# An adaLN transformer block planned by slots: GpSimd counted in the plan, one q product moved to the prologue, two stages of one unit later, fillers removed

## The chip, the cores and the metric

The kernel runs on one core of one Trainium2 chip. The time is the device time of one execution in microseconds, lower is better. Times "before" are the median of three runs. Engines: TensorE (PE, with its weight loads as PEld), VectorE (DVE), ScalarE (ACT), GpSimd (POOL), and SyncE (SP), which only issues DMAs here.

## What is computed

One block on x of shape (2, 1024, 128), 16 heads of 8 columns, a router over 8 experts with 64 hidden columns each:

```python
mod = (silu(c) @ wmod).reshape(2, 6, 1, 128)      # sa, ca, ga, sb, cb, gb; ga and gb kept away from 0
h = layernorm(x) * (1 + ca) + sa
q, k, v = heads(h @ qkv_w + qkv_b); q, k = rotary(q), rotary(k)
a = softmax(mask(q @ k.T / sqrt(8))) @ v           # causal
x = x + ga * (a @ out_w + out_b)
h = layernorm(x) * (1 + cb) + sb
onehot = one_hot(argmax(h @ w_router.T), 8)
u = leaky(h @ w_fc) ** 2                           # leaky: slope 0.5 below zero
x = x + gb * sum_e onehot_e * (u_e @ w_proj_e)
```

## The kernel before

The rows are cut into four units (b, half) of 512 rows, computed in the order (0,0), (0,1), (1,1), (1,0). Attention works on steps: a unit times a group of 4 heads, 16 steps in all. Step s has two passes. Pass A (`pass_a`, L968 and L973) makes score banks of 128 x 512 with q as rows, and VectorE reduces each to row maxima (`tmax`, L808). At the end of a step stage `max1` joins them (L738), GpSimd splits the negated maxima into three bf16 parts (`negp`, L486 to L489), and stage `max2` transposes these (PE L891), copies them (ACT L574) and writes them by three DMAs as extra rows of `qst`. Pass B (`pass_b`, L990) then makes the transposed scores with the maximum already subtracted, ScalarE takes the exponential (`exp`, L619), GpSimd zeroes the future of the diagonal tiles (`zero_future`, L515), and TensorE multiplies by v (`times_v`, L1010). Steps of a unit with half = 0 have 11 pass A banks, those with half = 1 have 27.

Before a unit's attention stand its preparation stages (`norm1`, `var1`, `nz`, `hT`, `q1` to `q3`, `k1` to `k3`, `v`, `load`): layer norm, transposition, the q and k products (PE L880), the rotation on VectorE (`rot`, L717), and `split`, which sums the two rotated parts (L355) and cuts the sum into three bf16 parts (L360 and L365, with copies on ScalarE at L562 and L566 between them). SyncE stores the parts to device memory after `q3` and `k3`, and `load` fetches them in the layout of the passes. After a unit's attention stand `n0` to `n3` (transpose and divide), `oT` and `out` (output product), `st` to `ln` (second layer norm), `h2`, `rt` (router), `a0` to `a3`, `m0` to `m3` and `y0`, `y1` (experts). `gates` (L494 to L496) multiplies the gates into the weights on GpSimd once, `xb` (L503) adds the gated bias to x there.

The function `plan` gives each pass A bank, each pass B bank and each stage a slot number. Every engine walks through the slots in order, and each stage issues its part in every engine's program, so a stage's slot is its place in each queue. TensorE does a stage one slot early. `put` moves a stage to a later slot when more than SIDES banks would be held; PREP_AT and POST_AT set starting slots by hand. The stages in `PRE` run ahead of slot 0. All passes and stages share seven PSUM banks in one round. Carried out for before, the plan puts pass A banks on slots 0 to 303 and pass B banks on slots 19 to 338.

`keep_warm` issues matmuls whose result nobody reads (L952, called fillers below): in the prologue, one in each slot before the first pass B bank, one in each slot of 304 to 338 (after the last pass A bank), and some in the last stages:

```python
if i < min(b_at):
    keep_warm(1)
...
if i > max(a_at) and i in b_at:
    keep_warm(1)
```

In unit (0,0) GpSimd does `split` for q and VectorE for k; in the other units GpSimd does both.

Of the kernel before, what the change touches and what calls it, by code (L numbers as in the profile page):

```python
# [29 lines left out]
P = 128  # L30
# [5 lines left out]
HALF = T // 2  # L36
# [35 lines left out]
def groups_b(half):  # L72
# [11 lines left out]
LEAD = 8  # L84
PVLAG = 3
SIDES = 2


HOLD = {"q1": 3, "k1": 3, "max2": 1}
BANKS_OF = {"mod": 1, "gate": 1, "hT": 1, "q1": 2, "k1": 2, "v": 1, "max2": 1, "oT": 1, "out": 1, "h2": 1, "rt": 1,  # L90
            "ohT": 1, "y0": 1, "y1": 1, **{f"n{g}": 1 for g in range(NG)}, **{f"a{c}": 1 for c in range(4)},
# [4 lines left out]
        "m2": 2, "y0": 1, "m3": 3, "y1": 4}  # L96

POST_LAST = ["oT", "out", "st", "var2", "ln", "h2", "rt", "a0", "a1", "ohT", "m0", "a2", "m1", "a3", "m2", "y0", "m3", "y1"]
PREP_AT = [[0, 0], [40, 1], [90, 1]]
POST_AT = {("out", (0, 0)): 79, ("a0", (0, 0)): 131}  # L100
MAX_LAG = 3
O_LAG = 3
GATES_AT = 22


WARM_PRE = {"start": 7, "mod": 8, "hT": 4, "v": 30}
# [1 line left out]
HIDDEN = ("a0", "a1", "a2", "a3")  # L108


PRE = [("mod", 0)] + [(name, (0, 0)) for name in ["norm1", "var1", "nz", "hT", "q1", "k1", "q2", "q3", "k2", "k3", "v"]] \
    + [("load", (0, 0), g) for g in range(NG)] + [(name, (0, 1)) for name in ["norm1", "var1", "nz", "hT"]] \
    + [("gate", 0)]


def plan():

    a_at, a_end, n = {}, [], 0
    for s, (b, half, g) in enumerate(STEPS):
        for job in bank_jobs_a(half):  # L120
            a_at[n] = (s, job)
            n += 1
        a_end.append(n)
    b_at, v_at, stages, held = {}, {}, {}, {}
    slot, v_end = 0, []
    for s, (b, half, g) in enumerate(STEPS):
        slot = max(slot, a_end[s] + LEAD)
        for gi, grp in enumerate(groups_b(half)):
            for bank in grp[3]:
                b_at[slot] = (s, gi, grp, bank, bank is grp[3][-1])  # L130
                slot += 1
            v_at[slot - 1 + PVLAG] = (s, gi, grp)
        v_end.append(slot - 1 + PVLAG)

    def put(at, *stage):

        need, hold = BANKS_OF.get(stage[0], 0), HOLD.get(stage[0], 2)
        if need and stage[0] in HIDDEN + ("y0", "y1") and stage[1][0:2] == UNITS[-1]:
            hold = 1
        while need and any(held.get(t, 0) + need > SIDES for t in range(at, at + hold)):  # L140
            at += 1
        for t in range(at, at + hold if need else at):
            held[t] = held.get(t, 0) + need
        stages.setdefault(at, []).append(stage)
        return at

    for s in range(len(STEPS)):
        put(a_end[s] - 1, "max1", s)
        put(a_end[s] + MAX_LAG, "max2", s)
        put(v_end[s], "o", s)  # L150
    put(GATES_AT, "gates", 0)
    done = {}
    for u, (at, more) in zip(PREPS[1:], PREP_AT):
        for name, gap in PREP.items():
            if (name, u) not in PRE:
                at = put(at + gap + more, name, u)
                if name == "k3":
                    done[u] = at
    for g in range(NG):
        at = a_end[1 + g] + MAX_LAG  # L160
        assert at > done[(0, 1)]
        put(at, "load", (0, 1), g)
        at = max(a_end[6 + g] + MAX_LAG, done[(1, 1)] + 1)
        assert v_end[4 + g] < at < a_end[7 + g] - LEAD
        for half in range(2):
            put(at, "load", (1, half), g)
    for s, (b, half, g) in enumerate(STEPS):
        at = put(v_end[s] + O_LAG, f"n{g}", (b, half))
        if g == 2:
            put(at + 1, "xb", (b, half))  # L170
        if g == NG - 1:
            for name in POST if (b, half) != UNITS[-1] else POST_LAST:
                at = max(at + POST[name], POST_AT.get((name, (b, half)), 0))
                for piece in range(len(PIECES[(b, half)])):
                    at = put(at, name, (b, half, piece))
    slots = max(list(a_at) + list(b_at) + list(v_at) + list(stages)) + 1
    return slots, a_at, b_at, v_at, stages, a_end


def adaln_block(nc, x, ct, wmod, wqkv, wsw, bcol, bv, wo, bo, wr, wfc, wpj, rope, out):  # L180
    slots, a_at, b_at, v_at, stages, a_end = plan()
# [24 lines left out]
    with ExitStack() as ctx:  # L206
# [6 lines left out]
        def sem(name):  # L213
            return ctx.enter_context(nc.semaphore(name))
# [7 lines left out]
        bv_sb = sb("bv_sb", [P, D])  # L222
# [66 lines left out]
        s_ldx = [sem(f"s_ldx{i}") for i in range(B * 2)]  # L289
        s_ldct, s_ldmod, s_ldqkv, s_ldbv = sem("s_ldct"), sem("s_ldmod"), sem("s_ldqkv"), sem("s_ldbv")  # L290
        s_ldrest = sem("s_ldrest")
        s_ident, s_mask, s_consts = sem("s_ident"), sem("s_mask"), sem("s_consts")
        s_one, s_ones, s_vones = sem("s_one"), sem("s_ones"), sem("s_vones")
        s_pool = sem("s_pool")
# [74 lines left out]
        def _(sp):  # L369
# [1 line left out]
            sp.dma_start(wqkv_sb[:, :], wqkv).then_inc(s_ldqkv, 16)  # L371
            sp.dma_start(wsw_sb[:, :], wsw).then_inc(s_ldqkv, 16)
            sp.dma_start(bcol_sb[:, :], bcol).then_inc(s_ldqkv, 16)
            sp.dma_start(rope_sb[:, :, :], rope).then_inc(s_ldqkv, 16)
            sp.dma_start(bv_sb[:, :], bv.partition_broadcast(P)).then_inc(s_ldbv, 16)
            for i in range(1, B * 2):
                sp.dma_start(xs[:, i], x[i]).then_inc(s_ldx[i], 16)
            sp.dma_start(bo_sb[:, :], bo.partition_broadcast(P)).then_inc(s_ldrest, 16)
# [56 lines left out]
        def _(pool):  # L435
# [36 lines left out]
            def run(st):  # L472
                name, u = st[0], st[1]
                if name in ("var1", "var2"):
                    rstd_of(st)
                if st == ("v", (0, 0)):
                    router_consts()
                if name in ("q1", "q2", "q3") or name in ("k1", "k2", "k3") and prep_no[u]:
                    split(pool, name, u)
                if name == "max1":  # L480
                    s, par = u, u % 2
# [149 lines left out]
        def _(dve):  # L631
# [58 lines left out]
            def run(st):  # L690
# [18 lines left out]
                if name in ("q1", "k1"):  # L709
                    i = (0, 1)[name == "k1"]  # L710
                    if name == "q1" and prep_no[u] == 0:
                        dve.wait_ge(s_ldqkv, 64)
                    if prep_no[u]:
                        dve.wait_ge(s_part[i], 3 * prep_no[u])
                    for j in range(2):
                        src, free = side_ready(dve, st, j)
                        dve.scalar_tensor_tensor(out=rot[i][:, j], in0=src, scalar=bcol_sb[:, 2 * i + j:2 * i + j + 1],  # L717
                                                 in1=rope_sb[:, j, HALF * u[1]:HALF * u[1] + HALF],
                                                 op0=ALU.add, op1=ALU.mult).then_inc(free, 1)
                if name in ("k1", "k2", "k3") and prep_no[u] == 0:  # L720
                    split(dve, name, u)
                if name == "v":
                    w = TU * (2 * u[0] + u[1])
# [90 lines left out]
        def _(pe):  # L814
# [30 lines left out]
            def run(st):  # L845
# [27 lines left out]
                if name in ("q1", "k1"):  # L873
                    i = (0, 1)[name == "k1"]
                    if i == 0:
                        pe.wait_ge(s_ldqkv, 64)
                    wait_read(pe, "hT", u)
                    for j, w in enumerate((wqkv_sb, wsw_sb)):
                        dst, full_ = fill(st, j)
                        pe.matmul(dst, w[:, D * i:D * i + D], ht[:, :], start=True, stop=True).then_inc(full_, 1)  # L880
# [139 lines left out]
            for i in range(slots):  # L1020
# [5 lines left out]
                    keep_warm(1)  # L1026
                if i in v_at:
                    times_v(*v_at[i])
                if i > max(a_at) and i in b_at:
                    keep_warm(1)  # L1030
                for st in pe_at.get(i, []):
                    run(st)
                    if i > max(b_at) and st[0] in WARM_POST:
# [48 lines left out]
```

## Time and profile before

| what | value |
|---|---|
| median of 3 runs | 392.32 us (389.57, 392.32, 393.1) |
| profiled execution | 389.84 us, span of its instructions 388.1 us |
| PE busy | 348.0 us (90% of the span) |
| DVE busy | 258.3 us (67%) |
| ACT busy | 215.9 us (56%) |
| POOL busy | 100.7 us (26%) |
| mean granted TensorE clock | 0.965 |
| chain that ended last | PE 68%, DVE 6%, issue 6%, POOL 6%, ACT 2% |

An engine's busy time says how much work it had, not whether it set the end. The granted clock is the share of TensorE's full speed that it was given: 1.00 is 2.4 GHz and 0.50 is 1.2 GHz. In a timeline the bracket at the end of a row is the idle time before it and what ended that.

### The profile page before, as it was taken

The page shows a single profiled execution, that of the slowest core. Times are in us where ns is not written, and L with a number is a line of the kernel's source. Part 1 is how long each engine was busy: PE and PEld are TensorE (multiplying, and loading weights), DVE is VectorE, ACT ScalarE, POOL GpSimd, SP SyncE. Part 2 cuts the span into 40 slices and gives each one's busy share as a digit, 9 for nine tenths or more (in the row PEclk, how much of TensorE's full clock was granted, in tenths as well). Part 3 has the DMA queues.
Part 4 walks back from the last instruction along what each step waited for, and adds up shares of the span by engine and source line. Part 5 has one row for each costly group of instructions (what it writes and reads, how often), then busy time and mean ns, then how long its engine had stood idle before and what let it go on. Part 6 is the DMA issues. An engine that isn't in the chain of part 4 may idle for free.

```text
span 388.1 us, 6918 instructions
## 1 busy us (share of the span) xinstructions
PE 348.0 (90%) x2350; PEld 166.9 (43%) x2383; DVE 258.3 (67%) x566; ACT 215.9 (56%) x415; POOL 100.7 (26%) x185
## 2 busy tenths in 40 slices
PE   6958779998688999899999889999999999999876
PEld 3435344443443343444543433444434444544544
DVE  3569478976986787668787684686887776213154
ACT  5251056664245586495576653854767666694333
POOL 4422184435410243300403011101114034213110
PEclk9989699999788999999999997999999999999999
DMA  7374212221030001510130400500000000000000
GB/s 242 124 224 130 69 44 62 65 62 69 22 83 0 3 1 68 139 28 0 65 88 3 122 2 1 125 0 29 1 2 5 1 3 4 1 1 2 29 0 29
DMA packets 12338, 18.87 MB, mean 49 GB/s; under 512 B 3600, under 2 KB 8592, under 8 KB 12176
## 3 DMA queue, kind: packets, MB, share of 16 engines
q1 hardware_dynamic: 12016, 18.04, 15.8%
q8 instruction: 20, 0.33, 0.4%
q10 hardware_dynamic: 288, 0.39, 0.3%
q14 instruction: 14, 0.11, 0.1%
HBM read 12.98 MB, written 5.24 MB: 47 GB/s over the span
## 4 chain that ended last, share of the span: by engine, by line
PE 68%; DVE 6%; issue 6%; POOL 6%; ACT 2%; SPq 1%; DMA 0%; ACTq 0%; POOLq 0%; DVEq 0%
PE ps_o L1010 17%; PE ps L973 15%; PE ps L990 13%; PE ps L944 4%; PE ps L931 4%; DVE tmax L808 3%; PE ps L880 3%; PE ps L952 3%; PE ps L898 2%; PE ps L968 2%; PE ps L912 1%; PE ps L937 1%; POOL pt L515 1%; PE ps L919 1%; DVE rot L717 1%
## 5 line engine op out<-in xcount | busy, mean ns | idle before, releaser
L808 DVE TENSOR_REDUCE tmax<-ps 128x1 f32<-128x512 f32 (+3 forms) x304 | 187.4, 657 | 71.3 <-PE ps L973 70.7
L619 ACT ACTIVATE pt<-ps 128x512 f32<-128x512 f32 (+1 forms) x304 | 162.8, 575 | 109.4 <-PE ps L990 107.8
L973 PE MATMUL ps<-kst,qst 72*128 72x128 bf16 (+3 forms) x576 | 115.6, 281 | 5.1 <-issue 2.9
L990 PE MATMUL ps<-qst,kst 75*128 75x512 bf16 (+3 forms) x384 | 113.6, 329 | 2.2 <-DVE tmax L808 1.3
L1010 PE MATMUL ps_o<-pt,v_sb 128*32 128x512 f32 (+3 forms) x768 | 83.6, 507 | 4.7 <-POOL pt L515 3.2
L973 PEld LDWEIGHTS ps<-kst,qst 72*128 72x128 bf16 x576 | 50.7, 101 | 71.2 <-ACT pt L619 21.0
L515 POOL TENSOR_SCALAR_AFFINE_SELECT pt<-pt 128x512 f32<-128x512 f32 x64 | 40.2, 637 | 78.7 <-ACT pt L619 78.4
L990 PEld LDWEIGHTS ps<-qst,kst 75*128 75x128 bf16 x384 | 35.4, 98 | 21.9 <-DVE tmax L808 4.1
L952 PE MATMUL ps<-maska,identb 128*128 128x512 bf16 x106 | 34.4, 404 | 3.4 <-POOL maska L452 3.3
L1010 PEld LDWEIGHTS ps_o<-pt,v_sb 128*32 128x32 f32 x768 | 15.6, 109 | 35.3 <-ACT pt L619 19.5
L486 POOL CAST negp<-negm 128x16 bf16<-128x16 f32 x16 | 3.2, 198 | 94.8 <-DVE negm L738 94.8
L470 POOL TENSOR_TENSOR rstd<-veps,mhalf 128x4 f32<-128x4 f32 (+1 forms) x9 | 8.5, 952 | 44.3 <-DVE veps L681 44.3
L952 PEld LDWEIGHTS ps<-maska,identb 128*128 128x128 bf16 x115 | 11.7, 103 | 19.3 <-ACT pt L619 5.0
L562 ACT ACTIVATE part<-full 128x512 bf16<-128x512 f32 x8 | 5.0, 628 | 26.7 <-POOL full L355 26.7
L355 POOL TENSOR_TENSOR full<-rot 128x512 f32<-128x512 f32 x7 | 8.9, 1266 | 38.2 <-DVE rot L717 37.6
L784 DVE TENSOR_TENSOR fg<-ps,fg 128x512 f32<-128x512 f32 (+1 forms) x20 | 11.4, 579 | 10.4 <-PE ps L937 5.6
L931 PE MATMUL ps<-h2t,wfc_sb 128*128 128x512 f32 (+1 forms) x40 | 17.6, 539 | 0.1
L944 PE MATMUL ps<-wpg,fg 128*128 128x128 f32 x128 | 15.9, 277 | 0.8 <-DVE fg L784 0.6
L968 PE MATMUL ps<-maska,identb 128*128 128x512 bf16 x40 | 16.2, 406 | 0.3 <-DVE tmax L808 0.2
L944 PEld LDWEIGHTS ps<-wpg,fg 128*128 128x128 f32 x128 | 15.3, 192 | 2.2 <-DVE y L791 0.9
L717 DVE SCALAR_TENSOR_TENSOR rot<-ps,bcol_sb,rope_sb 128x512 f32<-128x512 f32 x16 | 11.4, 744 | 3.2 <-PE ps L880 2.9
L747 DVE RECIPROCAL rden<-ps 128x16 f32<-128x16 f32 x16 | 4.0, 249 | 13.0 <-PE ps L898 13.0
(98 smaller groups left out, 273.9 us busy)
## 6 DMA issues: line engine op xcount, KB each, us to landing
qst<-qparts SPq DMA_DIRECT2D x48, 96.0 KB
kst<-kparts SPq DMA_DIRECT2D x48, 96.0 KB
qparts<-part SPq DMA_DIRECT2D x4, 384.0 KB, 2.6
kparts<-part SPq DMA_DIRECT2D x4, 384.0 KB, 2.6
xs<-in_x SPq DMA_DIRECT2D x4, 256.0 KB, 7.1
rope_sb<-in_rope SPq DMA_DIRECT2D x1, 1024.0 KB, 6.7
qparts<-part SPq DMA_DIRECT2D x4, 256.0 KB, 2.9
qst<-negt SPq DMA_DIRECT2D x48, 4.0 KB, 1.7
```

What stands on the lines that cost most here:

```text
L515: pool.affine_select(out=d, in_=d, compare_op=ALU.is_ge, fill=0.0, base=0, pattern=[[0, HG], [1, P]], channel_multiplier=-1).then_inc(s_tr ...
L619: act.activation(pt[:, G % NP, h0:h0 + nh, 0:w], src, ACT.Exp, scale=SCALE).then_inc(s_exp, 1)
L717: dve.scalar_tensor_tensor(out=rot[i][:, j], in0=src, scalar=bcol_sb[:, 2 * i + j:2 * i + j + 1], in1=rope_sb[:, j, HALF * u[1]:HALF * u[1 ...
L808: dve.tensor_reduce(dst, src, AX.X, ALU.max).then_inc(s_max, 1)
L880: pe.matmul(dst, w[:, D * i:D * i + D], ht[:, :], start=True, stop=True).then_inc(full_, 1)
L931: pe.matmul(dst[:, cols], wfc_sb[:, P * c:P * c + P], h2t[:, cols], start=True, stop=True).then_inc(full_, 1)
L944: last = pe.matmul(dst[:, D * t:D * t + D], fg[:, c, P * t:P * t + P], wpg[:, u[0], c], start=(c < c1), stop=(c == c1))
L952: pe.matmul(ps[:, reached[0] % NB, :], identb[:, :], maska[:, :, :].rearrange("p h k -> p (h k)"), start=True, stop=True)
L968: pe.matmul(dst, identb[:, :], maska[:, :, :].rearrange("p h k -> p (h k)"), start=True, stop=False, skip_group_check=True)
L973: last = pe.matmul(dst[:, j * nk:(j + 1) * nk], qst[0:ROWS, half, h, r * P:r * P + P], kst[0:ROWS, kh, h, k0:k0 + nk], start=(kind != "dia ...
L990: last = pe.matmul(dst[:, j * w:(j + 1) * w], kst[:, kh, h, kt * P:kt * P + P], qst[:, half, h, c0:HALF], start=True, stop=True)
L1010: last = pe.matmul(ps_o[32 * j:32 * j + 32, 0, c0:HALF], v_sb[:, TU * (2 * b + kh) + kt, c:c + 32], pt[:, G % NP, j, 0:HALF - c0], start=( ...
```

## The change

- `put` also keeps a set of slots in which GpSimd is taken: a stage named in the new table ON_POOL takes 2 slots (`gates` 4), and is moved later while one of them is taken (`max1` never moves).
- `q1` of unit (0,1), its q product, rotation and sum, is now the last stage of the prologue instead of slot 3. Its `q2` and `q3` come at slots 3 and 6 instead of 6 and 9.
- In the prologue VectorE does `split` for q as well as k; `k2` now stands ahead of `q3`; GpSimd makes the router constants earlier.
- `gates` moves from slot 22 to 28, behind the fourth group of step 0.
- `oT` of unit (0,0) is set to slot 81, and `out` follows (83); before they stood at 71 and 79. Through `put`, the preparation of (1,0) moves 2 slots later, that of (1,1) 3 to 6, `xb` (0,0) from 58 to 62, `k3` (0,1) from 21 to 23.
- The rope table is loaded in two halves with a semaphore each.
- The 35 fillers on slots 304 to 338 are removed. All passes keep their slots.

```diff
+ON_POOL = {"max1": 2, "q1": 2, "q2": 2, "q3": 2, "k1": 2, "k2": 2, "k3": 2, "var1": 2, "var2": 2, "xb": 2, "gates": 4}
...
-PREP_AT = [[0, 0], [40, 1], [90, 1]]
-POST_AT = {("out", (0, 0)): 79, ("a0", (0, 0)): 131}
+PREP_AT = [[0, 0], [40, 1], [93, 1]]
+POST_AT = {("oT", (0, 0)): 81, ("a0", (0, 0)): 131}
...
-GATES_AT = 22
+GATES_AT = 28
...
-PRE = [("mod", 0)] + [(name, (0, 0)) for name in ["norm1", "var1", "nz", "hT", "q1", "k1", "q2", "q3", "k2", "k3", "v"]] \
+PRE = [("mod", 0)] + [(name, (0, 0)) for name in ["norm1", "var1", "nz", "hT", "q1", "k1", "q2", "k2", "q3", "k3", "v"]] \
     + [("load", (0, 0), g) for g in range(NG)] + [(name, (0, 1)) for name in ["norm1", "var1", "nz", "hT"]] \
-    + [("gate", 0)]
+    + [("gate", 0), ("q1", (0, 1))]
...
+        busy = ON_POOL.get(stage[0], 0)
...
-        while need and any(held.get(t, 0) + need > SIDES for t in range(at, at + hold)):
+        while need and any(held.get(t, 0) + need > SIDES for t in range(at, at + hold)) \
+                or stage[0] != "max1" and any(t in pooled for t in range(at, at + busy)):
             at += 1
+        pooled.update(range(at, at + busy))
...
-    put(GATES_AT, "gates", 0)
     done = {}
...
+    put(GATES_AT, "gates", 0)
     for g in range(NG):
-        at = a_end[1 + g] + MAX_LAG
-        assert at > done[(0, 1)]
+        at = max(a_end[1 + g] + MAX_LAG, done[(0, 1)] + 1)
...
-            sp.dma_start(rope_sb[:, :, :], rope).then_inc(s_ldqkv, 16)
-            sp.dma_start(bv_sb[:, :], bv.partition_broadcast(P)).then_inc(s_ldbv, 16)
+            for half in range(2):
+                cols = slice(HALF * half, HALF * half + HALF)
+                sp.dma_start(rope_sb[:, :, cols], rope[:, :, cols]).then_inc(s_ldrope[half], 16)
+                if half == 0:
+                    sp.dma_start(bv_sb[:, :], bv.partition_broadcast(P)).then_inc(s_ldbv, 16)
...
-                if st == ("v", (0, 0)):
+                if st == ("q1", (0, 0)):
                     router_consts()
-                if name in ("q1", "q2", "q3") or name in ("k1", "k2", "k3") and prep_no[u]:
+                if name in ("q1", "q2", "q3", "k1", "k2", "k3") and prep_no[u]:
                     split(pool, name, u)
...
-                if name in ("k1", "k2", "k3") and prep_no[u] == 0:
+                if name in ("q1", "q2", "q3", "k1", "k2", "k3") and prep_no[u] == 0:
                     split(dve, name, u)
...
-                if i > max(a_at) and i in b_at:
-                    keep_warm(1)
```

## Rows read from the trace of the kernel before

**Rows 1.** The page's 40 slices, granted TensorE clock in tenths.

```profile
PEclk9989699999788999999999997999999999999999
```

**Rows 2.** Busy time of each engine in chosen stretches; behind POOL the granted clock.

```profile
228.00:231.80 3.80, 2.02 (x12) 1.07 (x11) 3.26 (x8) 2.21 (x4) 0.00 (x0) 0.99 0.00 0
25.70:30.20 4.50, 4.14 (x24) 2.97 (x26) 2.64 (x4) 0.78 (x1) 0.00 (x0) 0.63 0.74 182
37.80:41.38 3.58, 0.00 (x1) 0.00 (x1) 2.84 (x6) 0.63 (x1) 2.50 (x6) 0.88 0.02 9
41.38:47.20 5.82, 5.82 (x15) 2.69 (x16) 0.94 (x2) 0.27 (x1) 0.00 (x0) 0.50 0.32 109
97.70:100.56 2.86, 0.01 (x2) 0.03 (x1) 2.83 (x7) 0.63 (x1) 1.26 (x1) 1.00 0.00 0
100.56:109.00 8.44, 8.23 (x41) 6.20 (x43) 6.60 (x12) 2.10 (x4) 3.10 (x6) 0.60 0.31 89
231.80:238.40 6.60, 6.27 (x24) 2.99 (x26) 2.51 (x8) 1.34 (x3) 1.16 (x5) 0.50 0.00 1
```

**Rows 3.** Timeline of PE, 30 to 45 us.

```profile
30.65 1.02 PE L880 MATMUL ps<-ht,wqkv_sb 128*128 128x512 f32 x2
...
41.38 0.30 PE L891 MATMUL ps<-identb,negp 128*48 128x128 bf16 x1 [3.58 <-POOL negp L489]
...
42.86 1.92 PE L880 MATMUL ps<-ht,wqkv_sb 128*128 128x512 f32 x2
```

**Rows 4.** Timelines of POOL and DVE, 35 to 47 us.

```profile
35.14 1.26 POOL L355 TENSOR_TENSOR full<-rot 128x512 f32<-128x512 f32 x1 [10.76 <-DVE rot L717]
...
39.17 1.15 POOL L365 TENSOR_TENSOR part<-rot,part 128x512 bf16<-128x512 f32 x1 [0.81 <-ACT part L566]
40.27 0.20 POOL L486 CAST negp<-negm 128x16 bf16<-128x16 f32 x1
...
38.69 0.19 DVE L738 TENSOR_REDUCE negm<-tmax 128x16 f32<-128x32 f32 x1
...
46.95 0.69 DVE L808 TENSOR_REDUCE tmax<-ps 128x2 f32<-128x512 f32 x1 [3.58 <-PE ps L973]
```

**Rows 5.** Timelines of PE and DVE, 96 to 101 us.

```profile
100.56 0.63 PE L905 MATMUL ps<-ident,on 128*128 128x128 f32 x4 [2.85 <-DVE on L750]
...
96.04 0.56 DVE L808 TENSOR_REDUCE tmax<-ps 128x1 f32<-128x384 f32 x1 [1.88 <-PE ps L973]
```

**Rows 6.** Timeline of PE, times_v that waited.

```profile
55.16 1.07 PE L1010 MATMUL ps_o<-pt,v_sb 128*32 128x512 f32 x8 [0.81 <-ACT pt L619]
...
59.93 0.85 PE L1010 MATMUL ps_o<-pt,v_sb 128*32 128x384 f32 x8 [0.25 <-POOL pt L515]
...
75.51 1.07 PE L1010 MATMUL ps_o<-pt,v_sb 128*32 128x512 f32 x8 [0.69 <-POOL pt L515]
...
87.73 1.07 PE L1010 MATMUL ps_o<-pt,v_sb 128*32 128x512 f32 x8 [0.60 <-ACT pt L619]
...
91.44 0.85 PE L1010 MATMUL ps_o<-pt,v_sb 128*32 128x384 f32 x8 [0.61 <-POOL pt L515]
```

**Rows 7.** Groups by line, whole span: `split` on both engines.

```profile
L355 POOL TENSOR_TENSOR full<-rot 128x512 f32<-128x512 f32 x7 | 8.9, 1266 | 38.2 <-DVE rot L717 37.6 <-issue 0.6
...
L360 POOL TENSOR_TENSOR rot<-full,part 128x512 f32<-128x512 f32 x7 | 8.2, 1175 | 6.0 <-ACT part L562 6.0
...
L360 DVE TENSOR_TENSOR rot<-full,part 128x512 f32<-128x512 f32 x1 | 1.2, 1225 | 2.3 <-ACT part L562 2.3
...
L355 DVE TENSOR_TENSOR full<-rot 128x512 f32<-128x512 f32 x1 | 0.7, 693 | 0.1
```

**Rows 8.** The slots with a filler each: two stretches, and a filler in the chain.

```profile
339.50:349.20 9.70, 9.64 (x63) 3.98 (x61) 1.39 (x4) 9.31 (x19) 1.27 (x2) 1.00 0.00 1
326.00:363.00 37.00, 36.51 (x263) 17.89 (x266) 10.21 (x31) 24.61 (x49) 10.82 (x17) 1.00 0.01 2
...
348.05 0.22 PE ps L952
```

More of the change, by code:

```diff
@@ L123, in plan @@
         a_end.append(n)
-    b_at, v_at, stages, held = {}, {}, {}, {}
+    b_at, v_at, stages, held, pooled = {}, {}, {}, {}, set()
     slot, v_end = 0, []
@@ L158, in plan @@
                     done[u] = at
+    put(GATES_AT, "gates", 0)
     for g in range(NG):
-        at = a_end[1 + g] + MAX_LAG
-        assert at > done[(0, 1)]
+        at = max(a_end[1 + g] + MAX_LAG, done[(0, 1)] + 1)
+        assert at < a_end[3 + g] - LEAD
         put(at, "load", (0, 1), g)
@@ L291, in adaln_block @@
         s_ldrest = sem("s_ldrest")
+        s_ldrope = [sem(f"s_ldrope{i}") for i in range(2)]
         s_ident, s_mask, s_consts = sem("s_ident"), sem("s_mask"), sem("s_consts")
@@ L711, in run @@
                     if name == "q1" and prep_no[u] == 0:
-                        dve.wait_ge(s_ldqkv, 64)
+                        dve.wait_ge(s_ldqkv, 48)
+                    if name == "q1" and prep_no[u] < 2:
+                        dve.wait_ge(s_ldrope[u[1]], 16)
                     if prep_no[u]:
@@ L875, in run @@
                     if i == 0:
-                        pe.wait_ge(s_ldqkv, 64)
+                        pe.wait_ge(s_ldqkv, 48)
                     wait_read(pe, "hT", u)
```

## The prediction

> **What bounds the kernel now.** I began with the page: PE is busy for 90% of the span and carries 68% of the chain that ended last, so a microsecond counts only if it is PE's own work or time in which PE stands still. Then the granted clock by slices: it dips in four places [rows 1], and the table of stretches shows why. Each dip follows PE standing still. It stood for 3.58 us (37.80 to 41.38) and then ran 5.82 us at 0.50; it stood for 2.86 us (97.70 to 100.56) and the next 8.44 us had a mean of 0.60; it was busy for 2.02 of 3.80 us before 231.80 and then ran 6.60 us at 0.50 [rows 2]. At 0.50, which is 1.2 GHz, the same pair of matmuls takes 1.92 instead of 1.02 us [rows 3]. So a stall of PE is paid once for itself and again in the low clock behind it, and the reader should look at both. Last I read for each stall what ended it, in the timelines of PE, DVE and POOL.
>
> **First stall (37.8 to 41.4).** PE waits for `max2` of step 0, which waits for `negp` on POOL [rows 3]. DVE had the maxima at 38.69 + 0.19 = 38.88, but POOL stood in `q3` of (0,1) (39.17 to 40.32) and began `negp` at 40.27: 1.4 us late [rows 4]. The change takes this away: the sum (L355) that started at 35.14 [rows 4] moves to the prologue's end, `q2` and `q3` follow at slots 3 and 6, and POOL is done before the maxima. What is late next is DVE with its 11 reductions. Before, it did the two rotations of q (0,1) between them. Now these come first, when DVE has just finished the gate values. PE pays: the q product, four matmul passes, runs ahead of pass A in the stretch where the clock was 0.63 [rows 2], so 3.4 us by the low price instead of 1.9 [rows 3], and pass A's first bank starts some 2.7 us later. But three banks that ran at that low clock now run behind it, and bank 3, which stood behind the q product, starts at the same time within 0.4 us. DVE was idle for 1.86 of the 4.50 us before 30.20 [rows 2], and I estimate that it finishes bank 10 about 1 us sooner. In sum `max2` comes 1.4 + 1.0 + 0.3 = 2.7 us sooner, near 38.7, and PE stands still for about 1 us instead of 3.58.
>
> I take it that the low clock then stays away, since 0.81 us [rows 6] did not bring it. Its 5.82 us of work at 0.50 [rows 2] would be 2.9 us, but from 47 us on DVE paces, so I count what its bank 15 gains. PE's product k1 (0,1) and the banks before it take 3.1 instead of 5.1 us, so that bank's reduction, at 46.95 [rows 4], moves by 2.7 + 1.9 = **4.6 us**. Bounds: 0, if the later start of pass A eats the gain and the clock falls as before, and 5.8 us.
>
> **Prologue.** `split` for q on VectorE adds three operations there, about 3.1 us of DVE work (0.69 + 1.23 + 1.2, the third at the dearer of the two prices), but before this DVE waited 2.3 us for ScalarE's copies [rows 7]; the k parts come out within 0.5 us of their old time, the q parts about 1 us later, and their two stores with them. SyncE's loads of group 0 so start up to 1 us later. Nothing is lost, because PE now has the q product in front of pass A. If that cover were gone it would be the whole 1 us. Splitting the rope load adds one DMA issue to SyncE's queue, ahead of x of the later units, whose first reader is 20 us away: nothing.
>
> Here a rule and a row part. The sum L355 takes 1266 ns on POOL and 693 on DVE, but L360 takes 1175 and 1225 ns [rows 7]. The Trainium skill (GPSIMD Engine Reference, Engine selection) puts GpSimd about twice as slow for two-input elementwise work. This trace agrees for the first operation and not for the second. By the page the q parts would be out about 1 us sooner than I say, which changes nothing in the sum.
>
> **`k3`, `gates`.** At 55.16 PE had waited 0.81 us [rows 6]; the row names ScalarE, but the select on POOL came late behind `negp` and `k3` (0,1). With `k3` at slot 23 the select of slot 22 is ahead of it: −0.8. `gates` held the next selects back: 0.25 us at 59.93 [rows 6], −0.3 with what is in front of it. At slot 28 its 4.2 us lie between the last group of step 0 and the first of step 1 (slot 33). In front of `negp` of step 2 it may cost 0.3. **−1.1 us**, bounds −1.6 and +0.5.
>
> **Preparation of (1,0), `xb`.** The waits of 0.69 us at 75.51 (select behind `var1` on POOL) and 0.61 us at 91.44 (select behind `q2` and `xb`) go, and 0.60 us at 87.73 (select behind the sum of `q1`, which the row puts down to ScalarE) [rows 6]: 1.9 us. Bounds 0 and 1.9.
>
> **Second stall (97.7 to 100.6).** PE waited 2.85 us in `oT` for DVE's `n3` [rows 5]. With `oT` ten slots behind `n3` that wait goes. What is late next is DVE: it was busy for 2.83 of these 2.86 us [rows 2], and slots 62 to 78 have pass A only, 0.22 us of PE against over 0.6 us of DVE per bank. So PE's time there is DVE's, and `max2` of step 4 stands behind the same reductions. DVE gains its idle time of 1.88 us before 96.04 [rows 5] in large part (k1 (1,0) comes two slots later, and so two banks lie ready for it), and 0.6 us that it lost waiting for PE after the stall: −1.9. On the other side PE is idler than before, so the clock should fall here again, and `oT`, `out` and `v` at slots 81 to 83 meet it along with pass B: +0.9. **−1.0 us**, bounds −3.9 (with 3.4 us for a low clock that stays away) and +2.
>
> **Fillers.** A filler is 0.22 us of the chain [rows 8], so 35 are 7.6 us, with PE busy for 36.51 of 37 us. What takes their place is read in two parts. From 339.5 to 349.2 ScalarE is busy for 9.31 of 9.70 us [rows 8]; the eight fillers there return nothing (1.8 us). Two more losses are estimates from the order of the stages: the layer norm's chain in front of `h2` of (1,1) is longer than the work left to PE there, 0.5 us in the end, and the last groups wait for exponential and select, 1 us. ScalarE has 24.6 us of work in 37, so it doesn't pace the whole stretch. **−4.3 us**, bounds 0 and −7.6. The fillers in the last stages stay.
>
> **Sum.** 4.6 + 1.1 + 1.9 + 1.0 + 4.3 = 12.9 us from the profiled execution's 389.84 gives 376.9. From 131 us to 326 the slots are the same and PE is almost always busy, so what is gained ahead of it arrives at the end. The profiled execution was 2.5 us under the median of the runs, 392.32, and the runs spread over 3.5 us, about what one spell of low clock costs (6.6 us at 0.50). The median of the changed kernel should lie between 376.9 and 379.4: I predict **378.0 us**.
>
> **Rivals.**
> 1. *A shorter stall still brings the low clock* at 39 us, or a longer one follows at 98 us. Then the 1.9 us of the first part go, and up to 2 in the fourth: 380 to 383. For it: at 231.80 it fell after 3.80 us in which PE was busy for 2.02 [rows 2]. Against: 1 us is much shorter. Chance 0.18.
> 2. *ScalarE and the latency of exponential, select and product take the fillers' place.* PE then waits where it filled, and 1.5 us of the 4.3 remain: 380.8. For it: ScalarE's 9.31 us. Against: PE's other work in the stretch, 29 us, still exceeds ScalarE's 24.6. Chance 0.15.
> 3. *The low clock near 102 us stays away too*, or that at 231.80: each up to 3.3 us: 371.5 to 375. Chance 0.13.
> 4. *The front of the change moves stalls and removes none*: pass A starts 2.7 us later, DVE remains the pace, and only the fillers' 4.3 us and about 1 us of selects are gained: 384.5 to 387. Chance 0.11.
> 5. *Slower: without fillers the clock falls in the last attention stretch.* Waits of PE spread through slots 304 to 338, and the clock goes to 0.50 as at 231.80. Place: 326 us on. Price: 29 us of work take 29 us more if it holds throughout, 389.84 − 8.6 − 7.6 + 29 = 402.6; one spell costs 3.3 us and leaves the kernel faster. It decides the sign from the point at which the low clock covers more than twice the 12.9 us of the sum, 26 of the 62 us behind 326. The Trainium skill names this mechanism (TensorE: Matmul & The Clock Gate, A second HAM failure mode): a loop that cycles through PSUM banks can idle so often between groups that the clock oscillates. In this trace the clock stayed at full speed in all slices from 250 us on [rows 1], which is with the fillers, so it neither agrees nor disagrees. By that page this rival would be the likely one; I go by the little idle time that I expect. Chance 0.05.
>
> The forecast itself, 375 to 380, has 0.38.
>
> **How the numbers follow.** The range goes from rival 3's middle to rival 4's, 372.5 to 386: it leaves out about half of each and rival 5, 0.17. About 1% is what a measurement of this kernel can tell from no change, so the lines are 388.4 and 396.2. Faster: the forecast, rivals 1 to 3 and four fifths of 4 make 0.93, less 0.03 for an error in the base: 0.90. Slower: rival 5 less its single spells, 0.04. Within 1%: 0.06.
>
> **What would show it.** In the changed kernel's timeline PE L891 of step 0 stands near 39 us with about 1 us of idle time, and the clock at 1.00 from 31 us until about 98; no `times_v` waits for POOL around 55, 75 and 91 us; `oT` has no wait for DVE, but PE is idle near 95 us between pass A banks, with DVE full; the stretch from the last pass A bank to the last `times_v` is 4 us shorter. The prediction is wrong if the first idle time remains over 2 us, if pass A starts after 31 us, or if the clock goes below 1.00 behind the last pass A bank.

## The result, and the profile after

| kernel | median, us (lowest to highest) | runs | ratio to before |
|---|---|---|---|
| before | 392.38 (389.57 to 393.1) | 4 | |
| after | 387.26 (382.88 to 387.88) | 4 | 0.9862 [0.9814, 0.9911] |

The change gained 5 us where 14 were forecast, and the time lies above the range. The profiled execution took 387.2 us (span 385.5). In the ratios here and below, runs over 1.5% above the fastest of their kernel are left out, since spells of low clock come and go between executions; the medians are of all runs. The brackets behind a ratio are its 95% interval.

The page's slices of the granted clock, to be read beside [rows 1]:

```profile
PEclk9999987999889999999999987999999999997999
```

The dips of the prologue and behind step 0 are gone (slices 3 and 5 of before). Those near 102 and 230 us are still there; those in slices 6 and 7 and in slice 37, behind the last pass A bank, are new. The table of stretches shows what stands in front of each (columns: stretch and its length, busy us of PE, PEld, DVE, ACT, POOL with instruction counts, granted clock, DMA share, GB/s):

```profile
36.90:38.90 2.00, 0.05 (x1) 0.00 (x0) 1.97 (x6) 0.00 (x0) 0.83 (x4) 1.00 0.89 222
38.90:48.33 9.43, 8.26 (x48) 4.02 (x48) 7.73 (x16) 3.29 (x8) 3.28 (x7) 1.00 0.13 45
57.30:60.44 3.14, 0.07 (x1) 0.03 (x1) 0.64 (x2) 0.60 (x1) 3.14 (x6) 1.00 0.09 27
61.70:68.80 7.10, 7.10 (x37) 3.60 (x36) 3.71 (x8) 2.67 (x6) 0.63 (x1) 0.52 0.01 2
337.00:343.00 6.00, 6.00 (x43) 2.34 (x37) 0.55 (x2) 6.00 (x15) 0.63 (x1) 1.00 0.00 1
343.00:345.20 2.20, 1.22 (x10) 0.58 (x9) 1.38 (x2) 2.20 (x6) 0.63 (x1) 1.00 0.00 0
345.20:351.80 6.60, 6.51 (x30) 3.19 (x31) 0.69 (x1) 1.86 (x4) 1.22 (x2) 0.50 0.01 2
```

The stall of step 0 is down from 3.58 us [rows 3] to 1.96, and the 9.43 us behind it ran at 1.00, where before 5.82 us ran at 0.50, 1.2 GHz [rows 2]. But PE stands still between 57.3 and 60.4, with POOL busy for all of it, and the next 7.1 us run at 0.52. Near the end PE is busy for 1.22 of 2.20 us and then has 6.6 us at 0.50. Who is waited for stands in the timeline of PE (start, length, line, tiles, idle time before and what ended it):

```profile
25.73 0.63 PE L881 MATMUL ps<-ident,xn 128*128 128x128 f32 x4 [2.16 <-issue]
...
29.52 0.39 PE L978 MATMUL ps<-maska,identb 128*128 128x512 bf16 x1 [0.25 <-DMA kst<-kparts]
...
38.90 0.24 PE L901 MATMUL ps<-identb,negp 128*48 128x128 bf16 x1 [1.96 <-POOL negp L497]
...
60.44 0.43 PE L1020 MATMUL ps_o<-pt,v_sb 128*32 128x128 f32 x8 [3.07 <-POOL pt L523]
...
100.92 0.24 PE L901 MATMUL ps<-identb,negp 128*48 128x128 bf16 x1 [2.17 <-POOL negp L497]
...
345.29 1.51 PE L1020 MATMUL ps_o<-pt,v_sb 128*32 128x384 f32 x8 [1.07 <-POOL pt L523]
```

And POOL's own timeline in the new stall:

```profile
54.98 0.63 POOL L523 TENSOR_SCALAR_AFFINE_SELECT pt<-pt 128x512 f32<-128x512 f32 x1 [1.46 <-ACT pt L627]
55.58 0.45 POOL L502 TENSOR_TENSOR wog<-wo_sb,gate 128x128 f32<-128x128 f32 x1
...
58.46 1.25 POOL L504 TENSOR_TENSOR wpg<-wpj_sb,gate 128x512 f32<-128x512 f32 x1
59.67 0.63 POOL L523 TENSOR_SCALAR_AFFINE_SELECT pt<-pt 128x512 f32<-128x512 f32 x1
60.26 0.19 POOL L494 CAST negp<-negm 128x16 bf16<-128x16 f32 x1
```

`gates` runs from 55.58 to 59.71 (4.1 us), and in the queue behind it stand the select of step 0's last pass B bank and `negp` of step 2. So a sentence of mine in the section on the change is wrong, and so is the working that rests on it in the prediction: slot 28 is not behind the fourth group of step 0. That step's 11 pass B banks stand in groups on slots 19 to 22, 23 to 26, 27 and 28, and 29. Slot 28 is in front of the fourth.

I also counted one dip too few in before. Besides the four that the prediction names the clock is low at 119 to 123 us, behind a wait of PE of 0.92 us; in after it is not:

```profile
117.59 1.06 PE L919 MATMUL ps<-wr_sb,h2t 128*128 128x8 f32 x8 [0.92 <-ACT h2t L548]
```

Executions start at different times: the first transposition on PE stands at 8.89 us in before and at 10.97 in after, and between 8.9 and 11.2 in every kernel below, whatever was changed. I therefore count both from it. The transposition of `negp` (L891, now L901) of a step then comes, against before:

| | step 0 | 1 | 2 | 3 | 15 | end |
|---|---|---|---|---|---|---|
| before, us | 32.5 | 44.5 | 56.3 | 65.2 | 319.4 | 379.2 |
| after | −4.6 | −7.2 | −3.3 | −1.2 | −4.4 | −4.7 |

(Step 0: 41.38 − 8.89 = 32.49, 38.90 − 10.97 = 27.93.) 7.2 us were won by step 1, and 6 of them were lost again between step 1 and step 3, where `gates` stands. From step 15 to the end, where 4.3 us were forecast, 0.3 came. (Below, "end piece" is the window from the last `negp` transposition to the end.)

### The profile page after: what moved, and what is told of

Same layout as the page of the kernel before. It is cut to its first block, busy times and chain, and to the rows that moved or that the text cites. A ratio compares the mean times of both kernels' runs of the same rounds, so it can differ in the third digit from the quotient of the medians.

```text
span 385.5 us, 6882 instructions
## 1 busy us (share of the span) xinstructions
PE 348.8 (90%) x2348; PEld 164.8 (43%) x2348; DVE 260.3 (68%) x569; ACT 214.7 (56%) x415; POOL 96.8 (25%) x182
## 4 chain that ended last, share of the span: by engine, by line
PE 68%; issue 6%; DVE 6%; POOL 4%; ACT 4%; DMA 2%; SPq 1%; ACTq 0%; DVEq 0%; POOLq 0%
PE ps_o L1020 17%; PE ps L983 14%; PE ps L1000 14%; PE ps L954 4%; PE ps L978 3%; PE ps L941 3%; PE ps L890 2%; DVE tmax L818 2%; PE ps L908 2%; DMA qst<-negt 2%; DVE rot L727 1%; PE ps L947 1%; PE ps L929 1%; SPq L423 1%; PE ps L881 1%
## 5 line engine op out<-in xcount | busy, mean ns | idle before, releaser
L983 PE MATMUL ps<-kst,qst 72*128 72x128 bf16 (+3 forms) x576 | 114.4, 279 | 1.0 <-DVE y L801 0.3
L1020 PE MATMUL ps_o<-pt,v_sb 128*32 128x512 f32 (+3 forms) x768 | 85.5, 518 | 5.6 <-POOL pt L523 5.3
L983 PEld LDWEIGHTS ps<-kst,qst 72*128 72x128 bf16 x576 | 49.8, 100 | 67.8 <-ACT pt L627 17.4
L794 DVE TENSOR_TENSOR fg<-ps,fg 128x512 f32<-128x512 f32 (+1 forms) x20 | 11.4, 578 | 10.4 <-PE ps L947 8.5
L954 PE MATMUL ps<-wpg,fg 128*128 128x128 f32 x128 | 17.2, 292 | 0.6 <-DVE fg L794 0.6
L954 PEld LDWEIGHTS ps<-wpg,fg 128*128 128x128 f32 x128 | 16.4, 205 | 2.9 <-ACT pt L627 1.6
L360 POOL TENSOR_TENSOR full<-rot 128x512 f32<-128x512 f32 x6 | 7.6, 1265 | 29.2 <-DVE rot L727 29.2
L962 PEld LDWEIGHTS ps<-maska,identb 128*128 128x128 bf16 x80 | 8.4, 108 | 11.3 <-POOL maska L460 3.3
L589 ACT ACTIVATE ot<-ps_o 128x512 f32<-128x512 f32 x16 | 9.6, 599 | 5.8 <-PE ps_o L1020 5.8
```

What stands on the lines that cost most here:

```text
L794: dve.tensor_tensor(fg[:, c, cols], src[:, cols], fg[:, c, cols], ALU.mult).then_inc(free, 1)
L954: last = pe.matmul(dst[:, D * t:D * t + D], fg[:, c, P * t:P * t + P], wpg[:, u[0], c], start=(c < c1), stop=(c == c1))
L962: pe.matmul(ps[:, reached[0] % NB, :], identb[:, :], maska[:, :, :].rearrange("p h k -> p (h k)"), start=True, stop=True)
L983: last = pe.matmul(dst[:, j * nk:(j + 1) * nk], qst[0:ROWS, half, h, r * P:r * P + P], kst[0:ROWS, kh, h, k0:k0 + nk], start=(kind != "dia ...
L1020: last = pe.matmul(ps_o[32 * j:32 * j + 32, 0, c0:HALF], v_sb[:, TU * (2 * b + kh) + kt, c:c + 32], pt[:, G % NP, j, 0:HALF - c0], start=( ...
```

## The experiments

Line numbers shift between the kernels; operation and tiles tell the rows. "Counted from the start" means from the first transposition.

### `gates` and fillers, each alone

**a_gates34**: `gates` after all groups of step 0.

```diff
-GATES_AT = 28
+GATES_AT = 34
```

> The changed kernel with gates at slot 34, behind max1 of step 2 and the select of slot 33, with four slots until the next select. Theory: no select and no negp waits for gates, the stall at 60 us and its low clock go, and the 5.1 us that max2 of step 1 had gained arrive at the end: 380 to 382.5. Rival (VectorE paces, gates costs nothing): 387.

382.43 us, ratio 0.9743 [0.9698, 0.9787], 4.7 us below after. Its PE timeline has no wait where after has 3.07 us, and one of 0.91 us in the group behind:

```profile
57.68 0.43 PE L1020 MATMUL ps_o<-pt,v_sb 128*32 128x128 f32 x8
...
65.08 0.85 PE L1020 MATMUL ps_o<-pt,v_sb 128*32 128x384 f32 x8 [0.91 <-POOL pt L523]
```

The clock stays at 1.00 between 57 and 70 us. Counted from the start, step 3 now comes 6.3 us sooner than before and step 15 11.4, but the end only 9.2: the end piece has two dips. The forecast for this run, 380 to 382.5, held.

**a_gates29**: the same for slot 29, with `gates` taking 2 slots in the plan, since 4 would move it on.

```diff
-"gates": 4}
+"gates": 2}
-GATES_AT = 28
+GATES_AT = 29
```

> The changed kernel with gates at slot 29 instead of 28, so behind the select of step 0's last group instead of in front of it. Theory: gates (4.1 us on GpSimd) in front of that select made the new stall of 3.07 us at 60.4 and the low clock from 62 to 69 us behind it, about 6 us together, and so ate what the first stall had given back. At slot 29 that select is free, but gates now stands in front of negp of step 2 (slot 32), whose maxima are ready at 58: I expect the stall to move to that transpose, 2 to 3 us, and a time between: 383 to 386. Rival: the first stall's gain was lost to VectorE's pace and gates only filled idle time: 387, as the changed kernel.

385.13 us (378.19 to 387.65), too scattered for a ratio. The profiled execution, 381.0 us, has no stall for the select and no dip at 60 us; its longest wait there is 1.44 us, for `negp`, at 58.74, where I had expected 2 to 3. One slot is enough to be behind the select.

**a_fill**: after with the fillers.

```diff
+                if i > max(a_at) and i in b_at:
+                    keep_warm(1)
```

> The changed kernel with the 35 fillers of slots 304 to 338 put back, nothing else. From max2 of step 15 to the end the changed kernel took 59.5 us against 59.8 before, and the clock fell at 345 us. Theory: the fillers' 7.6 us went to waits for ScalarE and the select and to a spell of low clock, so putting them back gives the same time within 1.5 us, with the clock at 1.00 behind 326 us. Rival: the removal is worth its 4.3 us and the rest of the shortfall lies in front: 391.

386.72 us, ratio 0.9857 [0.9813, 0.9901]: the same as after. The clock of the end piece is 1.00 again, and that is worth as much as the 35 fillers cost.

**b_nofill**: before without them.

```diff
-                if i > max(a_at) and i in b_at:
-                    keep_warm(1)
```

> The kernel before with only the 35 fillers removed. Theory: same as before within 1.5 us (391 to 393), with a spell of low clock behind 326 us in the profile. Rival: 4.3 us faster (388). Third: the clock falls more than once and it is slower, 395.

392.87 us, ratio 1.0036 [1.0004, 1.0068]: nothing gained, some 1.4 us lost. The end piece, against 59.81 us at 1.00 in before:

```profile
328.08:391.10 63.02, 53.88 (x333) 30.18 (x332) 19.38 (x67) 31.24 (x70) 11.85 (x18) 0.86 0.03 9
```

PE has 27 matmul rows fewer (333 for 360) and is yet busy for longer, because two stretches ran at the low clock.

### With `gates` out of the way

**g34_fill**: a_gates34 with all fillers. **g34_fill3** and **g34_fill3b**: with every third, the first with the term `i % 3 == 0` (11 of the 35 slots), the second as here (12):

```diff
+                if i > max(a_at) and i in b_at and i % 3 == 1:
+                    keep_warm(1)
```

> The kernel with gates at slot 34, and the 35 fillers put back. Profiled, that kernel took 61.9 us from max2 of step 15 to the end, with two spells of low clock there; with the fillers the same piece took 59.8 us in two kernels, with none. Theory: the fillers pay for themselves, this is the fastest kernel so far, 379 to 381 (1 to 3 us under the one without). Rival: the two spells were chance and the fillers cost their issue time, 383 to 385.

> The kernel with gates at slot 34, and a filler only in every third of the slots 304 to 338 (12 of 35). If a third is enough to keep the clock, 377 to 379; if what counts is the few places where TensorE waits over 0.8 us, the spells come all the same and it is 382 to 384.

> As the kernel with a filler in every third slot (median 378.6, ratio 0.962), but in the slots with remainder 1 instead of 0. If twelve fillers keep the clock by their number, the ratio is the same within 0.006. If the first one only hit the right places by luck, spells of low clock come back behind 326 us and it is 381 to 383.

| kernel | median, us | ratio | end piece, us (clock) |
|---|---|---|---|
| before, 35 fillers | | | 59.81 (1.00) |
| g34_fill, 35 | 380.6 | 0.9706 [0.9669, 0.9742] | 59.88 (1.00) |
| g34_fill3, 11 | 378.63 | 0.9624 [0.957, 0.9678] | 56.89 (1.00) |
| g34_fill3b, 12 | 376.98 | 0.9606 [0.9563, 0.9648] | 56.99 (1.00) |
| a_gates34, none | 382.43 | 0.9743 [0.9698, 0.9787] | 61.92 (0.89) |

The same window in the profile of g34_fill3b:

```profile
319.61:376.60 56.99, 48.80 (x344) 26.68 (x343) 19.12 (x66) 31.07 (x70) 11.62 (x17) 1.00 0.03 10
```

With 12 fillers the longest wait of `times_v` in that stretch is 0.55 us (at 339.01), with none it is 1.07 (at 345.29 in after), and the clock holds. The two that keep every third are the fastest of all.

The 17 profiles, sorted by the fillers in the stretch from the last pass A bank to the last `times_v`, where they stand:

| fillers there | kernels | the stretch, us (clock) | low clock behind it |
|---|---|---|---|
| 35 | 10 | 39.2 (1.00) | in 3 (b_oT81, b_plan, b_split) |
| 11 or 12 | 2 | 35.9 and 36.0 (1.00) | in none |
| none | 5 | 38.0 to 38.3 (0.91) | in 4 (all but after) |

So within the stretch it is shown: all five profiles without fillers have low clock there, of the twelve with fillers none. The second dip of a_gates34 and b_nofill lies behind it, in the last stages. It comes with fillers too, so that removing them brings it is not shown; of the 61.92 us of a_gates34 it makes up 2.4. g34_fill beside a_fill prices slot 28 a second time: 0.9706 to 0.9857 is 5.9 us.

### The prologue and the first stall

**b_q1**: before with only the q product of (0,1) in the prologue (k1 kept at its slot).

```diff
-    + [("gate", 0)]
+    + [("gate", 0), ("q1", (0, 1))]
+                if (name, u) == ("k1", (0, 1)):
+                    at = 12
```

> The kernel before with q1 of (0,1) as the last stage of the prologue and q2, q3 three slots earlier (3 and 6), nothing else (split for q of (0,0) stays on GpSimd, k1 of (0,1) stays at slot 15, gates at 22, fillers in). Theory: this alone is the first stall's gain: max2 of step 0 moves from 41.4 to about 39, the low clock behind it stays away, 4 to 5 us: 387 to 388.5. Rival: the gain came from the shorter prologue (VectorE's split) and from the planner's spacing, and this edit gives under 2 us.

390.23 us, ratio 0.9934 [0.9894, 0.9974]: 2.6 us. The wait before `negp` falls to 2.00 us, but pass A starts 2.9 us later than in before, counted from the start, behind the old wait of PE in the prologue:

```profile
28.06 0.78 PE L873 MATMUL ps<-ident,xn 128*128 128x128 f32 x4 [4.18 <-issue]
...
42.20 0.30 PE L893 MATMUL ps<-identb,negp 128*48 128x128 bf16 x1 [2.00 <-POOL negp L491]
```

**b_split**: before with only the prologue's q parts on VectorE, `k2` ahead of `q3`, and the router constants earlier on GpSimd.

```diff
-"q1", "k1", "q2", "q3", "k2", "k3", "v"]] \
+"q1", "k1", "q2", "k2", "q3", "k3", "v"]] \
-                if name in ("k1", "k2", "k3") and prep_no[u] == 0:
+                if name in ("q1", "q2", "q3", "k1", "k2", "k3") and prep_no[u] == 0:
                     split(dve, name, u)
```

> The kernel before with the prologue of the change and nothing else: split for q of (0,0) on VectorE, k2 ahead of q3, router constants early. My prediction held this hidden only by the q product in front of pass A, with 1 us lost without it: 393. Rival: the 30 fillers of the prologue now end about 2 us later (23.6 instead of 21.5 in the traces), TensorE idles 2.2 instead of 4.2 us before hT of (0,1) and the low clock at 27 us stays away, which gains 1 to 2 us: 390.5.

390.86 us, ratio 0.999 [0.9954, 1.0027]: nothing. Its PE timeline says why:

```profile
26.05 0.63 PE L871 MATMUL ps<-ident,xn 128*128 128x128 f32 x4 [2.16 <-issue]
...
29.78 0.39 PE L968 MATMUL ps<-maska,identb 128*128 128x512 bf16 x1 [2.20 <-DMA kst<-kparts]
```

PE is through the prologue 2.0 us sooner (2.16 us of waiting for 4.18), and then waits 2.20 us for the load of `kst`. That is the cover of the prediction taken away: where the q product stands in front of pass A, the wait is 0.25 us (after, at 29.52).

**b_qs**: both edits together.

> The kernel before with q1 of (0,1) in the prologue and split for q of (0,0) on VectorE together, gates at 22, spacing and fillers as before. Theory: max2 of step 0 comes 4.5 us sooner, counted from the first transposition, as in the change (each alone gave 1.5), since only together do the loads and the q product leave no wait and the clock stay up; 385 to 387 at the end. Rival: they add up, 3 us: 389.

386.16 us, ratio 0.9863 [0.9837, 0.9888]: 5.4 us, where the parts alone give 2.6 and 0.4. Alone, each leaves low clock at 42 to 46 and at 55 to 60 us in its profile; together they leave none before 94 us. Counted from the start, step 0 comes 4.5 us sooner, as in after, and steps 1 to 3 come 7.1 sooner. From step 5 to the end it is 4.5 again: with the old wait at `oT` (2.86 us) in its place, the clock is low for longer behind it than in before (94 to 102 and 111 to 122 us, against 102 to 109 and 119 to 123). Why the split itself is shorter was not foreseen; the groups by line show it, first for b_plan (below, q's split on GpSimd as in before), then for after:

```profile
L365 DVE TENSOR_TENSOR rot<-full,part 128x512 f32<-128x512 f32 x1 | 1.2, 1227 | 2.3 <-ACT part L570 2.3
L370 DVE TENSOR_TENSOR part<-rot,part 128x512 bf16<-128x512 f32 x1 | 1.0, 1030 | 0.8 <-ACT part L574 0.8
```

```profile
L365 DVE TENSOR_TENSOR rot<-full,part 128x512 f32<-128x512 f32 x2 | 1.4, 689 | 0.2 <-ACT part L570 0.2
L370 DVE TENSOR_TENSOR part<-rot,part 128x512 bf16<-128x512 f32 x2 | 1.4, 688 | 0.2 <-ACT part L574 0.2
```

The same instruction takes VectorE 1225 ns in before [rows 7], where GpSimd works on q's parts, and 689 in after, where GpSimd is idle. It is so in all 17 profiles: 1.22 to 1.23 us in the six with q on GpSimd, 0.68 to 0.69 in the eleven others. The timelines of before show what GpSimd did meanwhile:

```profile
18.04 1.23 DVE L360 TENSOR_TENSOR rot<-full,part 128x512 f32<-128x512 f32 x1 [2.30 <-ACT part L562]
...
17.56 1.16 POOL L365 TENSOR_TENSOR part<-rot,part 128x512 bf16<-128x512 f32 x1 [0.81 <-ACT part L566]
18.65 0.52 POOL L459 MEMSET esel<- 8x512 bf16 x1
```

GpSimd's subtraction had 0.6 us left when VectorE's began, and VectorE's took 0.54 us longer than alone. So it looks as if the later one waits for the one under way, and not as if both run slower: that is my reading of the times, not shown by an experiment. The first sum on VectorE (15.04) began before GpSimd's next operation (15.45) and took its usual 0.69 us, while GpSimd's took 1.30 us for 1.15.

### The planner's part

**b_oT81**: before with only `oT` of (0,0) later (and through it `out` and the four stages behind). **g34f_oT71**: g34_fill with this edit undone.

```diff
-POST_AT = {("out", (0, 0)): 79, ("a0", (0, 0)): 131}
+POST_AT = {("oT", (0, 0)): 81, ("a0", (0, 0)): 131}
```

> The kernel before with oT of (0,0) at slot 81 and out at 83, with the four stages behind it 4 slots later, nothing else. Theory: the wait of 2.85 us before oT becomes a wait of nearly the same length before max2 of step 4, since VectorE's reductions pace slots 62 to 78, and the low clock follows as before: 391 to 392.5, a gain of at most 1 us. Rival: the wait goes and with it the low clock, 5 to 6 us: 386.

392.21 us, ratio 1.0002 [0.9975, 1.0029]. The wait of 2.85 us [rows 5] is gone and 3.11 stand at `max2` of step 4:

```profile
103.03 0.30 PE L891 MATMUL ps<-identb,negp 128*48 128x128 bf16 x1 [3.11 <-POOL negp L489]
```

> The kernel with gates at 34 and all fillers, with oT of (0,0) back ahead (73) and out at 79. Theory: TensorE waits for n3 or for negp of step 4 alike, as in the kernel before, so it stays at 380 to 382. Rival: with the front fast the early oT costs its wait and a longer spell of low clock, 383 to 385.

384.09 us, ratio 0.982 [0.9792, 0.9847], 4.4 us slower than g34_fill (0.9706; each against its own runs of before). In its PE timeline the old wait is back, and a second one follows at `v`:

```profile
94.85 1.09 PE L915 MATMUL ps<-ident,on 128*128 128x128 f32 x4 [3.10 <-DVE on L760]
...
106.18 0.39 PE L983 MATMUL ps<-kst,qst 72*128 72x512 bf16 x1 [1.15 <-DVE v_sb L737]
```

Between steps 3 and 5 g34_fill gains 4.3 us on before, counted from the start, and this kernel nothing. Behind 106 us it has low clock once more (0.68 over 106 to 122 us), and g34_fill, with 2.17 us of waiting at step 4, has 1.00 there. In the slow kernel the later `oT` spares no such spell: the clock falls again at 119 to 123 us in before and at 123 to 127 in b_oT81. So `oT` at 81 is worth nothing in the slow kernel and 4.4 us in the fast one.

**b_g34**: before with only `gates` at 34.

```diff
-GATES_AT = 22
+GATES_AT = 34
```

> The kernel before with gates at slot 34 instead of 22, nothing else. Where gates stood before, TensorE waited 0.25 us for the select behind it, so the move should give 0 to 1 us: 391 to 392. Rival: gates at 22 held more than the waits show, 3 us or more: 389 or less. It bounds what the new place of gates could have given the change at all.

393.59 us, ratio 1.0042 [1.0007, 1.0078]. Alone it gains nothing. Its profile has a longer dip at 119 to 130 us (0.61 over 118 to 131). It begins behind the wait of 0.92 us for ScalarE that before has too (117.59 there, 118.80 here), with a dip of 119 to 123; why it lasts longer here stays open. I had expected 391 to 392.

**g34_noq1**: a_gates34 without the q product in the prologue.

```diff
-    + [("gate", 0), ("q1", (0, 1))]
+    + [("gate", 0)]
```

> The kernel with gates at slot 34, with q1 of (0,1) back at slot 3; the planner then puts q2 at 6 and q3 at 12, behind max1 of step 0 instead of in front of it. Theory A: what cures the first stall is that q3 does not stand in front of negp, so either place of q1 does, and the time stays at 382 to 384. Theory B: the early rotation and sum in the prologue are what helps, and without them it is 386 or more.

385.88 us (380.62 to 388.76), ratio 0.9762 [0.9694, 0.9829]. Counted from the start it is 2.2 us sooner at step 0 where a_gates34 is 4.5 sooner; the ratios' intervals overlap, so the end can't carry a number.

**b_plan**: before with the planner's part alone: the table ON_POOL, `gates` at 34, `oT` at 81, PREP_AT; prologue, split and fillers as before. The rope table's load in two halves is in it too.

```diff
+ON_POOL = {"max1": 2, "q1": 2, "q2": 2, "q3": 2, "k1": 2, "k2": 2, "k3": 2, "var1": 2, "var2": 2, "xb": 2, "gates": 4}
-PREP_AT = [[0, 0], [40, 1], [90, 1]]
+PREP_AT = [[0, 0], [40, 1], [93, 1]]
-GATES_AT = 22
+GATES_AT = 34
...
+                or stage[0] != "max1" and any(t in pooled for t in range(at, at + busy)):
```

> The kernel before with the planner's part alone: ON_POOL, gates at 34, oT of (0,0) at 81, PREP_AT as changed; q1 of (0,1) stays at slot 3 (q3 comes at 12), split for q of (0,0) on GpSimd, fillers in. Theory: the spacing gives the part from max2 of step 3 to step 6 that no single part gives (3 to 4 us there), and a little at the first stall (q3 behind max1): 385 to 388. Rival: the spacing does nothing without the early q1, 390 to 392.

385.31 us, ratio 0.9851 [0.981, 0.9892]: 5.8 us. With the 5.4 us of b_qs that makes 11.2, and g34_fill, which has both, gained 11.5 (0.0294 × 391.76). The two halves add up within their intervals. Of this half `gates` and `oT` alone gave nothing (b_g34, b_oT81); the spacing alone was not run, so how the 5.8 us divide among them is not shown.

## Why the prediction was wrong

**The account.** Forecast and measured, in us against before:

| part | forecast | measured |
|---|---|---|
| first stall and prologue | −4.6 | −5.4 (b_qs) |
| preparation, `xb`, `oT`, `gates` out of the way | −4.0 | −5.8 (b_plan) |
| `gates` at 28 and not at 34 | +0.3 at most | +5.9 (a_fill beside g34_fill) |
| fillers | −4.3 | 0 (after beside a_fill) |

The sum of the right column is −5.3, and after gained 5.4 (0.0138 × 392.38). The intervals are 0.3 to 0.5% wide on each side, so each line is good to some 2 us; the two wrong ones are off by more. The removal of all fillers is 0 in this line and a loss of 1.5 us in a_gates34 beside g34_fill and of 1.4 in b_nofill.

**First failed step: `gates`.** I wrote that at slot 28 "its 4.2 us lie between the last group of step 0 and the first of step 1". The fourth group is one bank, on slot 29, and I had placed it in front of 28. So `gates` stands in front of a select of 0.63 us that PE needs, and PE paid 3.07 us for the wait and about 3.4 us (7.1 us at 0.52) for the low clock behind it. My 0.3 us were for `negp` of step 2, which also stands behind it; the select, which stands nearer, I had at nothing.

**Second failed step: the fillers.** The work was sized rightly. From the last pass A bank to the last `times_v` before took 39.2 us (323.76 to 363.00) and after 38.2 (322.15 to 360.35); 3.3 us of these are the low clock (6.6 us at 0.50), so without it the stretch would be 4.3 us shorter, and with 12 fillers it is 3.3 shorter (315.52 to 351.49). What failed is the assumption that PE stays full enough: it stood idle for 3.4 us of the stretch, with the fillers for 1.2. ScalarE is busy for 6.00 of the 6.00 us from 337, the select waited for it, `times_v` waited 1.07 us for the select at 345.29, and the clock fell. This is rival 5 in its mild form, single spells, which I had held to be worth 0.05 together with the rest. The Trainium skill (TensorE: Matmul & The Clock Gate, A second HAM failure mode) says, of a kernel of bf16 matmuls of 512 columns, that cycling through PSUM banks can leave enough short idle times between the groups for the clock to oscillate. The runs agree as far as the fall goes: the stretch is at 0.91 in all five kernels without fillers and at 1.00 in all twelve with them; it fell there once in each, and this stretch holds fp32 products as well. I had known it and set it aside for the little idle time that I expected.

**First stall: right in mechanism, its size near by luck.** `max2` of step 0 comes 4.6 us sooner counted from the start, where I said 2.7, the clock held, and the residual wait was 1.96 us where I said about 1. By step 1 it is 7.2 us, where I had 4.6 for a bank of that step; the 5.4 us of b_qs stand near my 4.6 only because part of the 7.1 is lost again at the second stall, which I had not reckoned with when I let the gain arrive whole at the end. The composition was off too. Pass A starts at the same time as before (18.6 against 18.7 us from the start) and not 2.7 us later, since the prologue is shorter and the q product ran at full clock. I let the q parts come 1 us late by taking 3.1 us for three operations on VectorE "at the dearer of the two prices"; they take 0.69 us each, and the prologue is 2.0 us shorter. The row of 1225 ns was true and was not VectorE's own price: it held with GpSimd at work beside it. The Trainium skill (GPSIMD Engine Reference, Engine selection) puts GpSimd about twice as slow for such work, and I let the row overrule it; for lines alone on their engine it holds here (1158 against 689 ns, 1265 against 692). The Trainium skill (GPSIMD Engine Reference, Specifications) says that GpSimd shares its SBUF interfaces with VectorE and contends with its instructions of two SBUF inputs; the pair 1225 and 689 agrees.

**Second stall: right in sign, too small.** As forecast the wait at `oT` went and DVE was next, with 2.17 us of idle time at `max2` of step 4. Alone that is worth nothing (b_oT81); in the whole it is 4.4 us, good to some 2 us, beside my bound of 3.9: I had priced one spell of low clock and not a second behind the wait at `v`. The selects (k3, (1,0), `xb`) were not measured singly; in after `times_v` waits once more for POOL, 0.47 us at 92.58, and not near 75.

**Rivals.** 1 did not happen at step 0; in after's profile a short dip (48 to 52 us) follows the wait of 0.68 us at step 1. 2 is not borne out in its price: with 12 fillers the stretch is 3.3 us shorter, and what took back the rest in after was the clock; its waits for ScalarE did come. 3 did not happen: the dips near 102 and 230 us remain in after. 4, which gives nearly the measured time, is refuted by b_qs and b_plan: the front did remove stalls. The time came out as it did because `gates` took 5.9 us back and the fillers gave none. (The range began at 372.5; the middle of rival 3 is 373.3.)

## What to carry to other kernels

Before a block of work is moved in an in-order queue, write down what stands behind it there slot by slot, the last short group too: 4.1 us of work that nobody waits for cost 5.9 us in front of a select of 0.63 us. Fillers are not to be kept or removed as a whole: read the clock of the stretch without them, and try every third, which here beat both. VectorE's price for an operation is to be taken from a row in which GpSimd is idle, and a part that is worth nothing alone (`oT` 0, VectorE's split 0.4 us) can be worth several us behind the others, so undo it in the fast kernel as well.

## What the runs showed that I had not expected

- VectorE's subtraction of 128x512 with two SBUF inputs takes 689 ns, and 1225 when it begins 0.6 us before the end of a GpSimd subtraction.
- Which wait brings the low clock is not told by its length: 0.84 us at 329.15 and 1.96 at 38.90 in after did not, 1.07 at 345.29 did. The wait of 0.68 us in front of step 1's transposition brought it in after and not in a_fill, whose program is the same up to there. The dips last from some 4 to 11 us, and the runs of one kernel spread by as much (378 to 388 us in a_gates29).
- The first transposition stands at 8.9 to 11.2 us by the execution and not by the kernel, so that spans alone can't tell 2 us apart.
